# Gates applied before the rows are stored, and fetches that add on chip: the tail of a graph layer with an expert layer behind it

## What is computed

```python
norm_src, norm_dst = rsqrt(max(out_deg, 1)), rsqrt(max(in_deg, 1))
agg = segment_sum((layernorm(x) @ W)[src] * norm_src[src], dst)
x = x + relu(agg * norm_dst + b)
# the expert layer: 8 experts, the best two of each token
p = softmax(layernorm(x) @ Wr + br); top_p, top_idx = top_k(p, 2)
w = top_p / top_p.sum()                      # the two gates of a token
y = gelu(xe @ W1[e] + b1[e]) @ W2[e] + b2[e] # xe: normed token, ln_g[e], ln_b[e]
out = x + w[0] * y[top_idx[0]] + w[1] * y[top_idx[1]]
```

## Time and profile before

| | us |
|---|---|
| median of three runs | 1667.14 |
| the profiled execution | 1664.14 |
| its span in the trace | 1662.7 |
| busy: PE, DVE, ACT, POOL | 1195.6, 951.2, 594.8, 1123.3 |
| granted TensorE clock, mean | 0.82 of full speed |

### The profile page before, as it was taken

How to read it: one execution, slowest core, us unless ns; L and a number is a source line. 1 busy time by engine, 2 the same in 40 slices (tenths; PEclk the granted TensorE clock), 3 DMA queues, 4 the chain that set the end, 5 groups by cost and what they waited for, 6 DMA issues and landing times.

```text
span 1662.7 us, 26613 instructions
## 1 busy us (share of the span) xinstructions
PE 1195.6 (72%) x9098; PEld 987.7 (59%) x9098; DVE 951.2 (57%) x2502; ACT 594.8 (36%) x1169; POOL 1123.3 (68%) x1116
## 2 busy tenths in 40 slices
PE   6954565647358545995499649969849768689995
PEld 5954344535146224982498439858728746578894
DVE  8997456656434353656265735764745648455552
ACT  4954011111032003440344025515315335455662
POOL 5006777777777777777777777777777757864233
PEclk9999565657578557996799779979959968899998
DMA  6027866775475447974787469769569579999982
GB/s 187 1 101 266 263 220 209 223 241 171 125 265 161 108 118 262 310 222 131 260 275 251 137 224 313 254 203 303 172 199 300 163 240 243 281 308 269 278 250 61
DMA packets 196730, 356.06 MB, mean 214 GB/s; under 512 B 25476, under 2 KB 94630, under 8 KB 196596
## 3 DMA queue, kind: packets, MB, share of 16 engines
q1 hardware_dynamic: 130008, 205.39, 36.7%
q0 software_dynamic: 60224, 142.57, 30.0%
q10 hardware_dynamic: 6364, 6.40, 1.2%
HBM read 290.80 MB, written 65.38 MB: 214 GB/s over the span
## 4 chain that ended last, share of the span: by engine, by line
PE 34%; DMA 26%; POOL 19%; issue 10%; DVE 7%; ACT 3%; SPq 0%; POOLq 0%; DVEq 0%; ACTq 0%
DMA gt<-zt,srcI 13%; PE ps L1260 9%; POOL gt L830 8%; PE ps L1159 8%; PE ps L1245 8%; DMA out<-gt,toks 5%; POOL xs L858 5%; DMA out<-acc 3%; POOL out L890 2%; PE ps L1134 2%; PE ps L1170 2%; DVE ohl L1334 2%; PE ps L1197 2%; POOL S L877 2%; DMA xb<-xs 1%
## 5 line engine op out<-in xcount | busy, mean ns | idle before, releaser
L830 POOL DMA_INDIRECT gt<-zt,srcI x832 | 834.2, 1003 | 254.1 <-issue 176.7
L1159 PE MATMUL ps<-gt,S 128*128 128x257 f16 x1664 | 349.3, 332 | 204.3 <-DMA gt<-zt,srcI 202.7
L1159 PEld LDWEIGHTS ps<-gt,S 128*128 128x128 f16 x1664 | 202.8, 151 | 306.4 <-DMA gt<-zt,srcI 291.2
L1245 PE MATMUL ps<-xe,w1b 128*128 128x256 f16 x2688 | 343.4, 282 | 34.5 <-DVE xe L1650 16.8
L1260 PE MATMUL ps<-w2b,hT 128*128 128x256 f16 x2688 | 316.7, 275 | 15.9 <-DVE yb L1682 8.2
L1245 PEld LDWEIGHTS ps<-xe,w1b 128*128 128x128 f16 x2688 | 270.0, 101 | 77.5 <-issue 20.0
L1106 ACT ACTIVATE h<-ps,cb 128x256 f32<-128x256 f32 x448 | 227.1, 557 | 245.9 <-PE ps L1245 244.8
L1656 DVE SCALAR_TENSOR_TENSOR hT<-h,cb,hT 128x512 f16<-128x512 f32 x224 | 167.7, 750 | 234.8 <-ACT hT L1110 234.2
L1260 PEld LDWEIGHTS ps<-w2b,hT 128*128 128x128 f16 x2688 | 264.7, 99 | 50.8 <-issue 15.7
L1110 ACT ACTIVATE hT<-h,cb 128x512 f16<-128x512 f32 x224 | 161.7, 722 | 7.3
L1084 ACT ACTIVATE aT<-ps 128x256 f32<-128x256 f32 x98 | 37.4, 381 | 319.5 <-PE ps L1190 319.5
(11 more groups left out here) (261 smaller groups left out, 1249.6 us busy)
## 6 DMA issues: line engine op xcount, KB each, us to landing
w1b<-ws SPq DMA_DIRECT2D x56, 1024.0 KB, 6.5
w2b<-ws SPq DMA_DIRECT2D x56, 1024.0 KB, 8.7
ws<-w2b SPq DMA_DIRECT2D x16, 1024.0 KB, 4.9
xb<-xs SPq DMA_DIRECT2D x56, 260.0 KB
gt<-zt,srcI POOLq DMA_INDIRECT x832, 4.0
ys<-yb SPq DMA_DIRECT2D x34, 256.0 KB, 7.0
w1b<-in_L_ffn_W SPq DMA_DIRECT2D x8, 1024.0 KB, 8.5
hT<-in_L_ffn_W SPq DMA_DIRECT2D x8, 1024.0 KB, 12.9
```

The lines of the kernel that those rows point to most:

```text
L830: e.indirect_dma_start(out=gt[:, i % NG, :], out_offset=None, in_=zt, in_offset=bass.IndirectOffsetOnAxis(ap=srcI[:, c, r:r + 1].bitcast(u ...
L1159: inst = e.matmul(PS[r % 2][:, 0:257], S[:, r % NS, :, c], gt[:, i % NG, part * 257:part * 257 + 257], start=(c == 0 and part == 0), stop= ...
L1245: inst = e.matmul(UP[n % 2][:, z * BS:(z + 1) * BS], w[:, l, kk, j * 128:(j + 1) * 128], xe[m % 2][:, k, kk, :], start=(kk == 0 and l == 0 ...
```

## The change

1. The gates are applied in `y` for every block, before `st` stores it: three small operations and two scalings more for each of blocks 0 to 33. `st` and the reload of a token buffer (`ld`) now wait for that (`s_y`).
2. `cc`, its ring and `wts` are gone. The fetches go straight to the tile's row of `acc`: the first plain, the second with an add. A batch's first fetches are all listed before its second ones, with the next batch's first fetches between them. The first fetch now waits for the base writes of these rows (`s_base`), no longer for the last edge tile, and `sums` waits for the fetches.
3. The last two chunks are cut into groups of two tiles, not four: (41, 43), (43, 45), (45, 47), (47, 49).
4. `plan()` lists POOL's steps when its clock is nearer, holds fetches and scatters back for up to one guessed us ahead of a give or sums that is due, and has other guesses for their costs.

```diff
+STEPS = [4] * (len(ENDS) - 2) + [2, 2]
+PARTS_OF = [-(-(t1 - t0) // step) for (t0, t1), step in zip(CHUNKS, STEPS)]
...
 def fetch_stages():
-    yield [[("cg", t, (("POOL", 2.5),)), ("cc", t, (("DVE", 1.1),))] for t in range(TG)]
+    turn = [(0, 0)]
+    for b in range(NSUM):
+        turn += [(b + 1, 0)] * (b + 1 < NSUM) + [(b, 1)]
+    for b, i in turn:
+        yield [[("cg", (t, i), (("POOL", 1.9 if i else 1.3),))] for t in range(*SUMS[b])]
...
-                after(end, "y", m, (("DVE", 0.85 if m < M0 else 1.7),), lambda e: over(m, e))
+                after(end, "y", m, (("DVE", 1.7),), lambda e: over(m, e))
...
-        if max(s["chain"], s["base"]) > s["now"] or clock["POOL"] > s["now"] + 2.6:
+        if max(s["chain"], s["base"]) > s["now"] or clock["POOL"] > s["now"] + 0.5:
...
-            emit("sums", b, (("POOL", 1.3 * (SUMS[b][1] - SUMS[b][0])),), s["now"])
+            emit("sums", b, (("POOL", 2.0),), s["now"])
+            s["chain"] = clock["POOL"] + 3.0 + 1.1 * (SUMS[b][1] - SUMS[b][0])
...
-            emit("give", gives.popleft(), (("POOL", 3.4),), s["now"])
+            emit("give", gives.popleft(), (("POOL", 3.7),), s["now"])
+            s["chain"] = clock["POOL"] + 4.5
...
-        s["chain"] = clock["POOL"] + 5.0
...
-                if kind == "cg" and clock["POOL"] > s["now"] + 2.5:
+                if kind in ("cg", "xs") and (clock["POOL"] > s["now"] + 0.3 or (gives or batches) and s["now"] + 1.0 < max(s["chain"], s["base"]) + 1.0 < s["now"] + 2.0):
...
                 elif kind == "cg":
-                    t = arg
-                    if t == 0:
+                    t, i = arg
+                    b = next(b for b, (b0, b1) in enumerate(SUMS) if b0 <= t < b1)
+                    if t == i == 0:
                         e.wait_ge(s_pick, 1)
                         e.wait_ge(s_zero, 16)
-                        e.wait_ge(s_tile, R * CT)
+                        e.wait_ge(s_base, 16 * BASE_DMAS)
...
+                    if i == 0:
                         e.indirect_dma_start(
-                            out=fetched_rows(t, i), out_offset=None, in_=ys,
+                            out=row(t), out_offset=None, in_=ys,
...
+                    else:
+                        if t == SUMS[b][0]:
+                            e.wait_ge(s_cg[b], 16 * (SUMS[b][1] - SUMS[b][0]))
+                        e.indirect_dma_start(
+                            out=row(t), out_offset=None, in_=ys,
+                            in_offset=bass.IndirectOffsetOnAxis(ap=cidx[:, 1, t:t + 1].bitcast(u32), axis=0),
+                            compute_op=ALU.add).then_inc(s_cg[b], 16)
...
                 elif kind == "sums":
                     b0, b1 = SUMS[arg]
-                    e.wait_ge(s_comb, b1)
+                    e.wait_ge(s_cg[arg], 32 * (b1 - b0))
...
                 elif kind == "st":
                     m = arg
-                    e.wait_ge(s_yread, m + 1)
+                    e.wait_ge(s_y, m + 1)
...
-                    if m >= M0:
-                        e.wait_ge(s_yread, m + 1)
-                        for z in range(2):
-                            inst = e.tensor_scalar(o[:, z, :], o[:, z, :], gate[:, 2, z:z + 1], None, ALU.mult)
-                        inst.then_inc(s_y, 1)
-                elif kind == "cc":
-                    t = arg
-                    e.wait_ge(s_cg[t % NC], 32 * (t // NC + 1))
...
-                    then(e.tensor_scalar(row(t), fetched_rows(t, 0), wts[:, 0, t:t + 1], None, ALU.mult))
-                    e.scalar_tensor_tensor(out=row(t), in0=fetched_rows(t, 1), scalar=wts[:, 1, t:t + 1], in1=row(t),
-                                           op0=ALU.mult, op1=ALU.add).then_inc(s_comb, 1)
+                    e.wait_ge(s_yread, m + 1)
+                    for z in range(2):
+                        inst = e.tensor_scalar(o[:, z, :], o[:, z, :], gate[:, 2, z:z + 1], None, ALU.mult)
+                    inst.then_inc(s_y, 1)
```

More of the change, by code:

```diff
@@ L394, in step_job @@
                     s["read"] = arg
-                if kind == "cc" and any(arg == b1 - 1 for b0, b1 in SUMS):
-                    batches.append((end, [b1 - 1 for b0, b1 in SUMS].index(arg)))
+                if kind == "cg" and arg[1] and any(arg[0] == b1 - 1 for b0, b1 in SUMS):
+                    batches.append((end + 5.0, [b1 - 1 for b0, b1 in SUMS].index(arg[0])))
                 if kind == "nd2" and ends(arg) in (LAST - 1, LAST):
@@ L402, in step_job @@
                     s["routed"] = arg
-                chain.at = end + 2.0 if kind == "cg" else s["now"] if kind == "xs" else end
+                chain.at = s["now"] if kind == "xs" else end
                 job.at = max(job.at, end)
@@ L444, in plan @@
             s["asked"] = True
-            fetches.append(Job(fetch_stages(), s["now"], width=NC - 1))
+            fetches.append(Job(fetch_stages(), s["now"]))
         moved = step_edges()
```

50 lines of the change are left out of this document (11 added, 39 removed).

## The result

| | before | after |
|---|---|---|
| median of 20 runs, us | 1664.25 | 1672.51 |
| lowest and highest | 1658.88, 1670.69 | 1666.80, 1677.79 |
| profiled execution, and its span | 1664.14, 1662.7 | 1674.42, 1672.9 |

The ratio of after to before is 1.0042, 95% interval 1.0032 to 1.0053: the changed kernel is 0.42% slower, 8.3 us against the forecast of 17 us less. The direction is measured, since the interval leaves out 1; by the bound of 0.5% that the prediction set it still counts as no change.

A forecast was written before the change was run, and what follows sets the result against it. POOL bounds until 1338 us; then the chain of gives and sums ends together with the blocks. First give 1373 + chain 272.8 = 1645.8, plus 1.4 outside the span and 3.0 for the median: 1650 us, range 1637 to 1668.

The forecast's parts named there:

- my +3: POOL's edge fetches: 34 blocks' added scaling pairs cost 0.1 us a pair, +3 us, from a range of 0 to 17.
- The rival in which the scalings block POOL: Edge fetches: each added pair blocks POOL for its whole 0.61 us, 21 us in place of 3, time 1668; chance 0.08.
- 18 for them and the scatter: Last chunk: groups of two and no `cc` move its scatter 18 us earlier, bounds 10 to 25.
- 1407.6: Start of the last chunk's first `up`: 1427.1 + 3 - 18 - 4.5 us.
- the forecast was 1619.5: End of the blocks: first `up` at 1407.6, then 219.9 us less 8 to the last result.
- the first give comes 10 earlier, at 1373: Start of the chain: block 34's result and the first give come 10 us earlier (4 to 16): 1383.9 + 3 - 4 - 10 = 1372.9.
- All three signs by which the prediction was to be wrong: Tail: first give after 1380, a batch's second fetches holding POOL, or a reshuffled list putting a store or give behind something slow.
- I call these two equal: Chain: 0.6 us more for each of 41 adding fetches against closer-listed gives, about 0.6 us at some ten gives.
- 3 us for the DMA engines: Chain's length: 41 adding fetches load the full DMA engines, +3 us from a range of 0 to 21.
- 9 off for the gives of the end: End of the chain: loads end about 27 us earlier, so some five gives take 5.5 us, not 9; bounds 0 and -15.
- the chain starts no earlier: Chain: block 34's weights set its first `up`, and the chain swallows the last chunk's gain, 1664 us; chance 0.10.
- The dear adding fetch: POOL's list from 1345 us: adding fetches decide from 3.5 us each; at 4.5 the time is 1693; chance 0.10.

The follow-up runs named there:

- e18: Kernel before with gates in every block and a tile's two plain-fetched rows added on DVE, list unchanged: 1668.82 us, ratio 1.0019.
- e9: Changed kernel with each of its four sums adding one node tile instead of ten or eleven: 1655.24 us, ratio 0.9909 to the kernel before.
- e3: Kernel before with node groups of two tiles in the last two chunks and nothing else: 1656.64 us, ratio 0.9956.
- e14: Changed kernel with the planner's guess of y at 0.85 us for early blocks: 1908.50 us, ratio 1.0041 to the kernel before at 1900.02.
- e2: Changed kernel with node groups of four tiles again: 1672.58 us, ratio 1.0052 to the kernel before.
- e11: Kernel before with gates in every block, a tile's two plain-fetched rows added on DVE, and y guessed at 1.7 us: 1676.34 us, ratio 1.0045.
- e1: Changed kernel with block 33's downs listed before block 34 is begun: 1668.73 us, ratio 1.0043 to the kernel before.
- e10: e11 with groups of two and block 33's downs listed ahead of block 34: 1679.74 us, ratio 1.0057 to the kernel before.
- e4: Changed kernel with the second fetch of each tile plain, not adding: 1662.68 us, ratio 0.9992 to the kernel before.
- e12: Kernel before with only the planner's new listing rules and guesses for POOL: 1687.62 us, ratio 1.0103.
- e15: e13 with groups of two: 1913.79 us, ratio 1.0063 to the kernel before at 1900.02.
- e5: Same kernel as e9, in a session where the kernel before took 1899.14 us: 1895.33 us, ratio 0.9978.
- e8: Same kernel as e10, in a session where the kernel before took 1899.14 us: 1925.25 us, ratio 1.0140.
- e13: Same kernel as e18, in a session where the kernel before took 1900.02 us: 1903.98 us, ratio 1.0027.
- e16: e14 with POOL's old listing rules and guesses: 1914.73 us, ratio 1.0074 to the kernel before at 1900.02.
- e17: Same kernel as e18, in a session where the kernel before took 1918.98 us: 1927.40 us, ratio 1.0043.

## Why the prediction was wrong, point by point

**Part 1 held.** The last edge fetch was forecast 3 us later, at about 1340; it went out at 1338.22, and from 1335 to 1343 in the runs of other kernels, so the shift is within what repeats. With the list held fixed, e18 has 34 blocks' added operations on DVE (three small ones of 0.16 to 0.22 us each and a pair of 0.64 together) at 41.7 us in all, where I had 41, and its 782 edge fetches average 1000 ns, where the earlier trace rows has 998. POOL has no wait beyond 0.30 us in that stretch in either kernel. The time rose by 3.2 us, which is my +3 in size. But the mean issue gives only 2 ns times 782, 1.6 us, so that 0.1 us a pair on POOL was the reason is not shown, and the match may be luck. The rival in which the scalings block POOL, 1668 us, falls, though its time is the nearest to what was measured: it would have moved the last edge fetch to 1355.

The Trainium skill, page "SBUF — State Buffer", section "Who interferes with whom", has GpSimd block fully while a DVE operation in a two-port mode holds the port pair that they share. These rows show no such block at this grain: the 68 scalings take 21.7 us in all, which would be 28 ns more for each of the 782 fetches if all of it held POOL, and the mean rose by 2. Whether these scalings took such a mode, no run shows.

**Part 3 held alone, and for the blocks.** The last chunk's slots were ready at 1375.5 us, 21.6 earlier than before, where I had 18 for them and the scatter:

```profile
1375.29 0.17 DVE L1437 CAST slI<-slF 128x8 int32<-128x8 f32 x1
```

Its scatter came at 1387.48 us all the same (forecast about 1383), because POOL's list has it behind the nine late fetches and the first give. The first `up` of that chunk is this line of PE in order of time, where I had 1407.6 and the earlier trace rows has 1427.08:

```profile
1410.12 1.22 PE L1237 MATMUL ps<-xe,w1b 128*128 128x256 f16 x5 [3.04 <-issue]
```

The last block's result and its scaling are these lines of DVE:

```profile
1618.42 0.75 DVE L1672 SCALAR_TENSOR_TENSOR gt<-ps,cb,b2b 128x512 f32<-128x512 f32 x1 [4.31 <-PE ps L1252]
1619.20 0.62 DVE L1677 TENSOR_SCALAR gt<-gt,gate 128x256 f32<-128x256 f32 x2
```

It ends at 1619.8 us; the forecast was 1619.5. Some luck is in that: the first `up` came 2.5 us late, and from there to the end took 2.2 us less than I had. The chain, not the blocks, ends last, as I had said, and e9 showed it.

**The first step that failed: "the first give comes 10 earlier, at 1373".** It came at 1383.67, an error of 10.7 us. I had taken the order of the list around it as given. Here is PE in order of time in the changed kernel, where L1237 is `up` and L1252 is `down`:

```profile
1343.34 5.24 PE L1252 MATMUL ps<-w2b,hT 128*128 128x256 f16 x24
...
1351.14 1.47 PE L1237 MATMUL ps<-xe,w1b 128*128 128x256 f16 x12
...
1358.77 2.78 PE L1252 MATMUL ps<-w2b,hT 128*128 128x256 f16 x24
```

then DVE's results of blocks 33 and 34,

```profile
1364.48 0.75 DVE L1672 SCALAR_TENSOR_TENSOR yb<-ps,cb,b2b 128x512 f32<-128x512 f32 x1
...
1377.66 0.75 DVE L1672 SCALAR_TENSOR_TENSOR yb<-ps,cb,b2b 128x512 f32<-128x512 f32 x1
```

and SP's queue, with its largest wait from 1290 to 1400 us (engine, line, what it waited for: us in total, times, the longest):

```profile
1335.38 0.38 SPq L1010 DMA_DIRECT2D xb<-xs  x1
1359.11 0.38 SPq L1014 DMA_DIRECT2D w1b<-ws  x1
...
1366.63 0.49 SPq L979 DMA_DIRECT2D ys<-yb  x1
```

```profile
SPq L1014 <- PE ps L1237: 24.1, 2, 23.2
```

Chunk 6 is ready earlier and `y` is guessed longer, so the planner lists all four `up` of block 34 between the two `down` of block 33. Both are needed. In the lists of e3 and e14 (groups of two, old guess) and of e2 and e11 (groups of four, new guess) both `down` stand ahead of the first `up`; put into the planner of e3, the new guess alone gives the order of the changed kernel, by the list as worked out on the host. The second `down` runs at 1358.77 us, the result is out at 1364.48 (1323.2 before), its store at 1366.63 and POOL's first fetch at 1372.32. SP's wait of 23.2 us for PE, at a weight load ahead of the store, was over at 1359.11 and did not hold the store, which follows the gated result (1365.9) by 0.7 us. Block 34's result, at 1377.66, gained 2.3 us, and even these are lost: it was gated at 1379.1, and the give stood 4.6 us behind fetches that began late. All three signs by which the prediction was to be wrong came: a first give after 1380, second fetches that hold POOL, and a list that "puts a store or a give behind something slow". It gave the last neither a price nor a chance.

e3 shows that the arithmetic of the step was right for its part alone: 1371. (It also shows that an earlier start is not all gained, since the chain then lengthened by 7.5 us.) e1 shows that repairing the store does not repair the give. e10 and e11 show the rest: gates in every block, with the planner's guess of 1.7 us, push blocks 24 to 33 back by 5.5 us or more (8.6 or more in the changed kernel), and with groups of two block 34 is later still. The step failed on the two parts meeting in one list, not on the size of either.

**The second step that failed: "I call these two equal".** I set 0.6 us for each of 41 adding fetches, which was right (0.58), against a gain of 0.6 us at ten gives from tighter listing, took 3 us for the DMA engines, and took 9 off for the gives of the end. The end gave 6.2 of the 9. The other two are wrong:

- The adding fetches did not vanish under the gives' landing times. Only what is issued while a give lands is free, and the list put ten of them between two gives; with 1.84 us from one to the next they held the chain for 24.0 us. The adds' cost is 10.3 us of chain in the profiled pair, 8.2 of it in the first sixteen gives (4.8 in that one stretch, 24.0 against 19.2), and 0.50% or 8.3 us by the ratios (e4). My term was 3, with 21 as its upper end. In the adds' own places the plain fetches of e4 take 1.07 us, so that the add holds POOL 0.51 us longer there.
- The tight rules are no gain of 6 us. On the kernel before they cost 1.0% (e12). How much of that is in the changed kernel is open, since the mechanism seen in e12, gives between the scatters, is absent from it.

In the profiled execution the end is 27.1 us behind the forecast of 1645.8: 10.7 for the first give, 7.3 for the adds (10.3 where I had 3), 2.8 for the end, and 6.3 on the sums and first gives, which e4 has without the adds. One more term was off: I added 3.0 for the median above the profiled execution, from three runs; over twenty it is 0.1.

Two smaller pieces of the chain can be read in the table and the rows and are there without the adds too. The eight scatters, which before were issued while a `sums` landed (1395.93 to 1411.02 in the earlier trace rows), now stand between two gives, 14.5 us apart (1383.67 to 1398.20), where a give took 11 to 12. And the first three sums, which had none, six and six fetches issued behind them, now have nine, nine and seven, and take 20.2, 21.7 and 19.1 us instead of 15.1 to 17.9; with plain fetches (e4) they take 19.6, 19.8 and 19.2. Whether the fetches beside them are the reason stays open: in e3 a `sums` with six fetches beside it took 13.2 us and one with none 20.7.

One reading of the rows was off, without weight in the sum. The 17.6 us of the earlier trace rows are 7 waits of the 17 scalings of that group; over all 41 tiles there are 17 waits of 33.8 us.

**The rivals.** Nearest in what it says of the chain was "the chain starts no earlier", 1664 us at 0.10: the start was right, and its chain was 16 us too short. Its reason, block 34's weights, is not what the trace shows; the blocks ahead of it came late. The dear adding fetch decided from 3.5 us a fetch; it was 1.58, and yet the adds cost 8 us. About half of that fell on one stretch, so what counted for much of it was how many stood in front of a due give, and not only their sum against POOL's whole list. My forecast took 3 us from a range of 0 to 21 for the adds and nothing for the list, and so the range ended at 1668 where the time is 1672.5.

**What stays open.** The parts do not add: -0.44% (e3), +0.45% (e11), +0.50% (the adds, e4 against after) and +1.03% (e12) make +1.5%, and the changed kernel is at +0.42%. Each change of a guess reshapes the list, and the interplay was not taken apart further. It is open why e1, with its fetches 17.7 us earlier, is not faster in the median. The changed kernel with the old guess (e14) and the groups of two with early gates on the list of e3 (e15) were not tried while the kernel before took some 1665 us, and no run has the adding fetches alone on the kernel before.

## What to carry to other kernels

When a planner writes the order, an edit to one cost or one group size moves things far from it: price the new list, not the old list with faster parts, and above all the first link of the last chain. An operation moved to a queue is free only while that queue's chain is in flight, so count how many of them stand in a row in front of a due step. Try the parts singly first; here one was a gain alone (0.44%), and the package lost it.

## What was not expected of the hardware

- **The adding fetch.** An indirect fetch that adds into its destination holds POOL 1.579 us, a plain one of as many rows 0.995 (the groups above). The scatters with addition to `out` take 1.59 to 1.62 on the mean and the plain ones to `xs` 1.00, so the add is seen in the issue, whatever the destination. On the DMA engines the row of adding fetches in the changed kernel can be set against the same row in e4, where they are plain. POOL's queue (packets, MB, share of 16 engines) from 1428 to 1442 us of the changed kernel, then from 1427 to 1437 us of e4:

```profile
q0 software_dynamic: 1016, 1.01, 43.5%
```

```profile
q0 software_dynamic: 325, 0.87, 23.6%
```

  That is 6.0 us of all engines for a MB with the add and 2.7 without, with all queues together at 98% and 97% in both windows. A MB takes 2.7 times as many packets with the add, about 1 KB each instead of 2.7. The 6.0 are near the 6.8 of the sums of the earlier trace rows (1.44 MB, 61.3% of 16 us), and the 2.7 near the 3.1 of the plain fetches of the earlier trace rows (2.40 MB, 30.1% of 25 us). By these figures a fetch of 128 rows, 0.13 MB, costs the engines an estimated 0.8 us with the add and 0.35 without, 18 us more for 41. The upper end of 21 us in the prediction was thus near what the engines had to do more, and its 3 us far from what came of it.

- **The same kernel at two speeds.** In the sessions of e5 to e8, e13 to e16 and e17 the kernel before took 1899 to 1919 us, 14% more than the 1665 of the others; the chip with one and the same number was at 1919 in one session and 1670 in another. The window from 500 to 900 us, first of the kernel before at 1662.7 us, then of e17, which differs from it by the early gates only and took 1919.8:

```profile
500.00:900.00 400.00, 293.35 (x2238) 234.75 (x2237) 197.31 (x561) 122.47 (x225) 306.03 (x309) 0.80 0.66 210
```

```profile
500.00:900.00 400.00, 229.15 (x1658) 188.21 (x1658) 172.87 (x531) 89.65 (x164) 252.91 (x258) 0.77 0.53 164
```

  Every engine does less in the same 400 us, POOL 252.91 instead of 306.03, at nearly the same clock. POOL no longer bounds the edge tiles: it has waits of up to 11 us there, where it had none above 0.30, and the last edge fetch comes at 1547 us or later. In e17 the last two gives wait 2.45 and 3.00 us for their blocks. Short sums stood only 0.2% under the kernel before there (e5) and 0.9% in the other session (e9). Why is open: in e5, too, the chain ends last, some 26 us behind the last block's result, and the changed kernel with full sums was not run there. What sets the two speeds was not found in the traces. A verdict on a few per mille holds for the condition in which it was taken.
